# A unit's three query transfers issued at one place or at three, in a fused transformer block on one core

## The reference

```python
tp = _swiglu(time_emb @ w_t1 + b_t1) @ w_t2 + b_t2
shift1, scale1, shift2, scale2 = jnp.split(tp, 4, axis=-1)
h = _rmsnorm(x, g1) * (1.0 + scale1[:, None, :]) + shift1[:, None, :]
x = x + _mha(h, w_qkv, b_qkv, w_ao, b_ao, n_head)
h = _rmsnorm(x, g2) * (1.0 + scale2[:, None, :]) + shift2[:, None, :]
x = x + _ffn(h, w_fc, b_fc, w_fo, b_fo)
```

## Time and profile before

| | us |
|---|---|
| median of 3 runs | 3166.36 |
| lowest and highest of them | 3157.5, 3170.91 |
| the profiled execution's own time | 3172.68 |
| its span | 3170.5 |
| PE busy | 3046.1 (96%) |
| POOL busy | 1678.5 (53%) |
| stage B in it, from the first score of unit 0 to the first of unit 31 | 381.0 to 1932.9 |

### The profile page before, as it was taken

How to read it: one execution, slowest core, us unless ns; L and a number is a source line. 1 busy time by engine, 2 the same in 40 slices (tenths; PEclk the granted TensorE clock), 3 DMA queues, 4 the chain that set the end, 5 groups by cost and what they waited for, 6 DMA issues and landing times.

```text
span 3170.5 us, 39623 instructions
## 1 busy us (share of the span) xinstructions
PE 3046.1 (96%) x14977; PEld 2052.2 (65%) x14977; DVE 1862.9 (59%) x2970; ACT 1551.4 (49%) x2837; POOL 1678.5 (53%) x718
## 2 busy tenths in 40 slices
PE   7989899999999999999999999799999999999999
PEld 5777655555555554555555554578888888888887
DVE  4668687878788787888778775633333333222222
ACT  4333376767677676776767667332222232111111
POOL 4644578888888888888888887522222200000000
PEclk9999899999999999999999999899999999999999
DMA  6665489998999989999899898532222201221110
GB/s 234 222 185 158 134 189 192 188 206 180 195 191 189 202 174 196 194 184 203 175 198 191 190 209 174 141 107 80 80 80 80 73 21 40 75 83 56 54 54 27
DMA packets 172325, 460.07 MB, mean 145 GB/s; under 512 B 24020, under 2 KB 57896, under 8 KB 140200
## 3 DMA queue, kind: packets, MB, share of 16 engines
q0 software_dynamic: 32256, 234.90, 37.2%
q1 hardware_dynamic: 139352, 221.60, 23.3%
q10 hardware_dynamic: 528, 1.05, 0.1%
HBM read 141.86 MB, written 80.74 MB: 70 GB/s over the span
## 4 chain that ended last, share of the span: by engine, by line
PE 41%; POOL 25%; DMA 22%; issue 8%; DVE 3%; ACT 1%; SPq 0%; POOLq 0%; DVEq 0%; ACTq 0%
POOL b_acc L895 18%; DMA b_pt<-b_pt 16%; PE e_g L1569 11%; PE e_a L1569 11%; PE e_y L1580 10%; POOL b_acc L912 4%; DMA b_pt_last<-b_pt 3%; PE e_p L1514 2%; DMA b_pt<-b_pt_last 2%; POOL a_q_lo L366 2%; PE b_s L1002 2%; PE a_qk L561 1%; PE b_o L1050 1%; POOL a_yq L359 1%; PE a_tv L583 1%
## 5 line engine op out<-in xcount | busy, mean ns | idle before, releaser
L934 DVE TENSOR_REDUCE b_mpart<-b_m 128x1 f32<-128x512 f32 x1960 | 1200.0, 681 | 318.8 <-PE b_m L986 318.7
L881 ACT ACTIVATE b_pt<-b_s 128x512 f32<-128x512 f32 x1824 | 975.5, 601 | 402.9 <-PE b_s L1002 328.5
L895 POOL TENSOR_TENSOR b_acc<-b_acc,b_pt 128x2048 f32<-128x2048 f32 x200 | 931.3, 4656 | 216.3 <-DMA b_pt<-b_pt 197.5
L1002 PE MATMUL b_s<-b_qs,b_ks 98*128 98x512 f32 x2048 | 854.7, 420 | 24.0 <-ACT b_pt L881 12.7
L986 PE MATMUL b_m<-b_ks,b_qs 96*128 96x512 f32 x1960 | 761.3, 408 | 0.0
L1002 PEld LDWEIGHTS b_s<-b_qs,b_ks 98*128 98x128 f32 x2048 | 391.7, 192 | 346.1 <-issue 181.2
L986 PEld LDWEIGHTS b_m<-b_ks,b_qs 96*128 96x128 f32 x1960 | 376.2, 192 | 129.4 <-DVE b_mpart L934 56.2
L1050 PE MATMUL b_o<-b_pt,b_vg 128*32 128x512 f32 x3648 | 447.5, 603 | 0.0
L1449 DVE SCALAR_TENSOR_TENSOR e_u_lo_f<-e_a,keep_chan,e_u_lo_f 128x512 f32<-128x512 f32 x128 | 96.1, 751 | 543.8 <-PE e_a L1569 543.8
L1569 PE MATMUL e_g<-e_h_hi,e_w 128*128 128x512 f32 x1024 | 338.8, 392 | 14.3 <-DVE e_h_lo L1393 8.1
L1569 PE MATMUL e_a<-e_h_hi,e_w 128*128 128x512 f32 x1024 | 337.8, 391 | 0.0
(11 more groups left out here) (152 smaller groups left out, 3438.8 us busy)
## 6 DMA issues: line engine op xcount, KB each, us to landing
b_pt<-b_pt POOLq DMA_DIRECT2D x175, 1024.0 KB, 8.5
b_pt<-b_pt_last POOLq DMA_DIRECT2D x25, 1024.0 KB, 8.0
b_pt_last<-b_pt POOLq DMA_DIRECT2D x24, 1024.0 KB, 8.4
scratch_qk_hi<-a_q_hi SPq DMA_DIRECT2D x64, 256.0 KB
scratch_qk_lo<-a_q_lo SPq DMA_DIRECT2D x64, 256.0 KB
b_qs<-scratch_qk_hi SPq DMA_DIRECT2D x64, 256.0 KB, 6.9
b_ks<-scratch_qk_hi SPq DMA_DIRECT2D x28, 512.0 KB, 6.8
scratch_v<-a_vsb SPq DMA_DIRECT2D x32, 256.0 KB, 2.7
```

Of the source, the lines that this page charges most:

```text
L881: act.activation(tile(u, kt)[:, h, :], ps_s[:, score_place(i) % LEAD, :], ACT.Exp, scale=SCALE).then_inc(p_ready, 1)
L895: pool.tensor_tensor(acc[u % 2][:], acc[u % 2][:], tile(u, 2 * n + 3), ALU.add).then_inc(pool_added, 1)
L934: dve.tensor_reduce(mpart[n % 2][:, i // 4, i % 4:i % 4 + 1], ps_m[:, at, :], AX.X, ALU.max).then_inc(max_done, 1)
L1002: pe.matmul(ps_s[:, place % LEAD, :], ks[n // NJ % 2][0:QR, h, kt * P:(kt + 1) * P], qs[n % 4][0:QR, h, :], start=True, stop=True).then_in ...
```

## The change

`load_queries` gets a list of the rows that it is to load, and the per-unit list of SP issues them one at a time: the first behind the output's store, the second behind the wait for the third value product, ahead of piece 0, and the third behind a new wait for the fifth value product, ahead of the wait for the sixth and piece 1. The queries of units 0 and 1, which stage A loads, are issued together as before.

```diff
-    def load_queries(sp, u):
+    def load_queries(sp, u, rows=range(3)):
         G, c, i = u // NJ, u % NJ, u % 4
-        for r, src in enumerate((qk_hi, qk_hi, qk_lo)):
+        for r in rows:
+            src = qk_lo if r == 2 else qk_hi
             sp.dma_start(f32(qs[i][r * HD:(r + 1) * HD, :, :]), src[0, G, :, :, c * TB:(c + 1) * TB]).then_inc(q_in[i], 16)
...
             sp.wait_ge(st_done, STEPS * (u + 1))
-            if u + 2 < UNITS:
-                load_queries(sp, u + 2)
             if u:
                 store_output(sp, u)
+            if u + 2 < UNITS:
+                load_queries(sp, u + 2, (0,))
             sp.wait_ge(pv_done, NK * u + RING - 1 + 3)
+            if u + 2 < UNITS:
+                load_queries(sp, u + 2, (1,))
             load_piece(u, 0)
             head["sync"](sp, u, 0)
+            sp.wait_ge(pv_done, NK * u + RING - 1 + 5)
+            if u + 2 < UNITS:
+                load_queries(sp, u + 2, (2,))
             sp.wait_ge(pv_done, NK * u + RING - 1 + 6)
             load_piece(u, 1)
```

## The result

The changed kernel takes 3182.07 us (median of 6 runs, 3177.58 to 3183.58), the one before 3164.77 us on the same chip: ratio 1.0046, 95% interval 1.003 to 1.0063. It is slower by 14.6 us by the ratio and 17.3 us by the medians, where 3156.4 was forecast, with 3141 to 3177 as range.

The account below looks back on a forecast made before the run. Stage B was taken as bound by PE near its limit, held up by POOL's adds and folds. Fold 5's -2.8 and the third query's +1.4 net -1.4 us per group, taken as -10: 3156.4 us, range 3141 to 3177.

Parts of the forecast that it names:

- What bounds the kernel: Stage B: PE near its limit; POOL's adds and awaited folds delay tile 8, making long units, mostly at place 1; 51 us winnable.
- The relief of fold 5: At a unit's start: two of four transfers leave fold 5, -0.7 us per start, ends 0 and -1.1.
- the third query's cost on L1: Fold 1's landing time (L1), zero to +1.0 us; taken +0.6, +0.1, +0.4, +0.3 at places 0 to 3 of a group.
- The second query: Issued at 14 us beside fold 6, ahead of piece 0: nothing, -0.5 to +0.5, hidden by 1.7 us of slack.
- The sum: Per group of four units: -2.8 for fold 5, +1.4 for the third query, net -1.4 us; -10 over 7.5 groups.
- The third one: Rival, chance 0.12: third query and piece 1 together burden folds 0 and 1; +2.2 us a group, +17, 3183 us.
- The first rival: Nothing changes, chance 0.22: fold 1 loses what fold 5 gains, DMA work stays the same; 3166 us, give or take 5.
- The second rival: The long units go, chance 0.20: shorter backlog at place 1 spares two or three the slow clock; -25 us, 3141.
- Queries late at tile 10: Rival, chance 0.03: third query lands too late for tile 10, PE stands 1 us in 22 units; +12, 3178 us.
- Fold 5 to 8.6: Announced sign: fold 5's mean landing time falls from 9.3 to about 8.6 us.
- Fold 1 at place 0 to 10.9: Announced sign: fold 1's landing time at place 0 rises from 10.3 to about 10.9 us.
- Fold 6 to stay: Announced sign: fold 6's landing time stays as it was.

Follow-up runs that it names:

- e1: Against the kernel before: only the third query moved, to the fifth value product ahead of piece 1; first and second stay ahead of the output's store. 3187.4 us, ratio 1.0070.
- e2: Against the kernel before: only the second query moved, to the third value product ahead of piece 0; first and third stay at the unit's start. 3176.56 us, ratio 1.0027.
- e3: Against the kernel before: all three queries still together at the unit's start, but issued behind the output's store. 3161.56 us, ratio 0.9981.
- e7: Against the kernel before: queries loaded for unit u+3, not u+2; two behind the output's store, the third behind the denominators. 3154.27 us, ratio 0.9963.
- e4: Against the change: third query issued behind piece 1 instead of ahead of it. 3189.07 us, ratio 1.0068 to the kernel before.
- e6: Against the kernel before: output's store first, then all three queries behind the first value product. 3156.81 us, ratio 0.9968.
- e12: Against e7: the two queries at the unit's start wait for the first value product. 3152.25 us, ratio 0.9954 to the kernel before.

## Why the prediction was wrong

**What bounds the kernel** was right: the stalls grew at tile 8, behind POOL's add, and the long units are those at place 1.

**The relief of fold 5** was too small in the sum and wrongly explained. -0.7 a start was taken, -2.8 a group; measured were -1.6, -0.8, -0.5 and -0.9, together -3.8, beyond the lower end of -1.1 at place 0. The prediction gave it to the two queries that leave the unit's start, by proportion. But e1 and e2, which each take one query away and leave the store behind the rest, have fold 5 at 9.3 and 9.1 us on average against 9.2 before, while e3, which takes none away, has it at 8.1 and the change at 8.2. So the relief comes from the output's store going first, a step that the prediction costed at nothing; that the term came near to its size was luck.

**The step that failed is the third query's cost on L1.** It said "zero to +1.0 on L1" and took 0.6 + 0.1 + 0.4 + 0.3 = 1.4 a group. With the third query moved alone (e1), L1 rose by 2.9 a group, by 1.5 at place 0 and 1.7 at place 2, both beyond the stated upper end. The bound was wrong in kind, not only its size: it took a fold to be late by no more than the 1.0 us that the moved transfer is worth. What e1 shows in its place is that the fold meets more than that transfer: fold 0 stayed at 9.0, but piece 1 at place 0 landed 30.4 us after the unit's start in place of 27.9, so more of its 512 KB lay beside fold 1, which is issued at 23.6. That this push is all of the 1.5 us is argued from these averages, not tested. The prediction named the push ("it pushes piece 1 onto fold 1") and priced it too low.

**The second query** was costed at nothing, between -0.5 and +0.5, "hidden by the slack" of fold 6. Wrong: e2 has it at +9 us. Fold 6 did keep its slack, but piece 0 behind the query reached into fold 0 (+2.3 at place 0), and L1 rose by 1.8 a group. At place 0 the second query and piece 0 had landed by 21.6 us on average, before fold 1 is issued at 23.0, so fold 1 got their delay at second hand: from fold 0 ahead of it in the folds' queue, or from piece 1, which landed at 30.0 in place of 27.9. The runs do not separate these two. The Trainium skill, "DMA: Bandwidth & Descriptors", section "Queues, rings and completion order", says, in its paragraph on the queues of SP and ACT, that on each DMA engine descriptors are consumed in ring order. For the folds, which go through GpSimd's queue, the traces show the same order of landing: in none of the fourteen does a fold land ahead of one issued before it, and the closest two are 4.2 us apart.

In the change, with both queries moved and the store first, L1 rose by 2.1, 0.8, 1.1 and 0.4, together 4.4, and L3 by 0.9 more.

**The sum** becomes, with the measured terms, -3.8 + 4.4 + 0.9 = +1.5 us a group, +11 us over 7.5 groups, against some 15 to 17 timed. The rest is not accounted for.

**The rivals.** The third one, the third query and piece 1 together on folds 0 and 1 with 3183 us, is what happened, at 3182; it had 0.12. Its condition, that L1 rises by more than L5 falls at places 0 and 1, holds at place 0 (2.1 against 1.6); at place 1 the two are equal (0.8). The price it gave L1, 3.0 a group, is too small against 4.4, and its L5 relief, 0.8 a group, far too small against 3.8; L3 was left out. That 3183 is so near is luck in part: its net of +2.2 a group is more than the measured +1.5. The first rival (the work is shared, so nothing changes) is out: the DMA share of stage B was 0.89 to 0.93 in all traces, 0.91 in the change as before, and yet thirteen orders of the same transfers span 0.9954 to 1.0079. Nothing here speaks against the interleaving itself; what falls is the conclusion that the place of a transfer makes no difference. The second rival needed shorter backlogs and shows in e7, not in the change. Queries late at tile 10 did not occur in the change: no such wait is among its waits. They did in e4, where the third query is issued behind piece 1.

**The signs announced.** Fold 5 to 8.6: reached, 8.2 on average. Fold 1 at place 0 to 10.9: it went to 12.4. Fold 6 to stay: it fell from 11.0 to 9.3. ACT's wait to fall to 48: it rose to 81.1, the sign named for the third query taking over.

## What to carry to other kernels

Price a moved transfer by the chain of awaited transfers that it lands among, including those behind the one it touches, and with the transfers that it pushes back in its own queue, and look at what is issued next to its new place; the same split was +0.46% with one neighbour and -0.49% without it. "Spread out" is no aim in itself: the best places here were those where the transfers in flight had slack (beside fold 6, until e6 used that up, and for one query beside the even chain), and a plain swap of two issues (e3) gave a gain that the split then lost. If a buffer is free a stage earlier, use it to pick the place, as e7 and e12 do.

## What the runs showed of the hardware

How long PE stands does not by itself tell what clock it is granted afterwards. In the change's unit 21 PE stood 5.5 us in sum, in pieces of at most 2.5 us, and the granted clock stayed 1.00 with 49.3 us busy; in units 13 and 17 PE stood 3.4 to 3.5 us in sum, nearly all in one piece, and the clock over the unit was 0.94 (6.8 us of it at 1.2 GHz in place of 2.4) with 51.6 us busy. All three units took 55 us. That looks as if pieces were cheaper than one long stall, but single pieces do not order that way: in unit 2 of the kernel before, one of 2.37 us was followed by the slow clock (0.97 over the unit), while one of 3.21 us in its unit 22 and one of 2.99 us in the change's unit 9 were not (1.00 in both). PE's timelines, units 2 and 22 before:

```profile
508.69 1.07 PE L969 MATMUL b_s<-b_acc,keep_ones 128*32 128x512 f32 x8 [2.37 <-ACT b_pt L881]
...
1508.02 1.06 PE L969 MATMUL b_s<-b_acc,keep_ones 128*32 128x512 f32 x8 [3.21 <-ACT b_pt L881]
```

The prediction's second rival, which lets the slow clock follow once PE stands some 3 us, is therefore not a rule that these traces bear out.
